# The key compare of the adjacency tiles reads its ramp from PSUM instead of SBUF

## What is computed

```python
h = typed_linear(feat[src], W, etype)
att = jax.nn.sigmoid(jax.nn.leaky_relu(h_l + h_r, NEG_SLOPE)) * edge_weight[:, None]
msg = h3.transpose(0, 2, 1) * att[:, None, :]
agg = jax.ops.segment_sum(msg, dst, num_segments=n_nodes)
```

```python
Wh = h @ W + b
base = adj_v * sc * no_diag            # one number per edge
prop_pos = segment_sum((base * sim_pos)[:, None] * Wc, row)
prop_neg = segment_sum((base * sim_neg)[:, None] * Wc, row)
out = scale * (coeff[0] * prop_pos + coeff[1] * prop_neg + coeff[2] * Wh)
```

## Time and profile before

| | |
|---|---|
| time, median of 3 runs | 4748.81 us (4748.74 to 4754.69) |
| profiled execution: its own time | 4738.92 us |
| profiled execution: its span | 4736.4 us |
| TensorE busy | 3146.4 us (66%) |
| VectorE busy | 3140.1 us (66%) |
| GpSimd busy | 3231.1 us (68%) |
| ScalarE busy | 1567.6 us (33%) |
| mean granted TensorE clock | 0.844 of 2.4 GHz |

### The profile page before, as it was taken

The page is one execution under the profiler, slowest core; times in us unless marked ns, Lnnn a source line. Parts: engine busy times, 40 slices in busy tenths (PEclk is TensorE's granted clock), DMA queues, the critical chain, the costliest instruction groups (busy, mean ns, idle before and its releaser), DMA issues. The chain is left out here.

```text
span 4736.4 us, 63536 instructions
## 1 busy us (share of the span) xinstructions
PE 3146.4 (66%) x16141; PEld 1881.8 (40%) x16141; DVE 3140.1 (66%) x5194; ACT 1567.6 (33%) x3248; POOL 3231.1 (68%) x3224
## 2 busy tenths in 40 slices
PE   2576777777777777776555655555476767676778
PEld 2344454554455455444343443444232222322222
DVE  4677776767777677775655555554477767676787
ACT  2422232323232232323411211221344545444434
POOL 0277777777777777775377777777676777775546
PEclk6798888988888888897877777777689989889999
DMA  1233333323233332333322222222355545455556
GB/s 53 97 92 97 91 96 91 101 88 99 91 95 94 91 98 91 98 92 88 103 66 72 78 66 71 80 68 66 112 156 143 163 128 163 134 156 140 177 163 191
DMA packets 355160, 502.05 MB, mean 106 GB/s; under 512 B 92987, under 2 KB 214844, under 8 KB 354669
## 3 DMA queue, kind: packets, MB, share of 16 engines
q1 hardware_dynamic: 251549, 394.52, 25.3%
q0 software_dynamic: 100352, 102.96, 10.7%
q10 hardware_dynamic: 2896, 0.59, 0.1%
HBM read 290.63 MB, written 207.16 MB: 105 GB/s over the span
## 5 line engine op out<-in xcount | busy, mean ns | idle before, releaser
L809 POOL DMA_INDIRECT frows<-messages,fidx x2352 | 2280.6, 970 | 847.8 <-issue 669.3
L889 PE MATMUL fps_b<-hot_key,hot_lo 128*128 128x343 f32 x3136 | 1238.6, 504 | 406.4 <-PEq L70 403.7
L948 DVE TENSOR_TENSOR strip<-strip,fps_b 128x343 f32 x1568 | 787.7, 502 | 546.1 <-DVEq L70 521.6
L824 ACT ACTIVATE turned<-fps_t 128x512 f32<-128x512 f32 (+1 forms) x754 | 431.6, 572 | 1742.7 <-ACTq L70 1738.1
L879 PE MATMUL fps_sum<-hot,frows 128*64 128x80 f32 x4704 | 551.5, 302 | 600.1 <-PEq L70 600.1
L1118 POOL DMA_INDIRECT lrows<-messages,lidx x784 | 743.3, 948 | 294.5 <-issue 222.6
L889 PEld LDWEIGHTS fps_b<-hot_key,hot_lo 128*128 128x128 f32 x3136 | 544.8, 207 | 728.3 <-issue 676.3
L879 PEld LDWEIGHTS fps_sum<-hot,frows 128*64 128x64 f32 x4704 | 522.8, 195 | 691.1 <-issue 691.1
L918 DVE TENSOR_SCALAR hot_key<-iota_f,edge 128x343 f32<-128x343 f32 x1574 | 753.2, 479 | 0.1
L1284 ACT ACTIVATE pos<-l_c,coeff 128x896 f32<-128x896 f32 x392 | 394.4, 1006 | 597.6 <-PE l_c L1179 596.8
L1179 PE MATMUL l_c<-unit_t,unit_g 64*128 64x448 f32 x1568 | 437.2, 636 | 133.5 <-DVE acc L1107 72.4
(11 more groups left out here) (183 smaller groups left out, 1880.0 us busy)
## 6 DMA issues: line engine op xcount, KB each, us to landing
adj<-turned SPq DMA_DIRECT2D x696, 256.0 KB
edge<-adj SPq DMA_DIRECT2D x294, 448.0 KB
adj_x<-adj SPq DMA_DIRECT2D x98, 448.0 KB
frows<-messages,fidx POOLq DMA_INDIRECT x2352, 2.4
messages<-msg SPq DMA_DIRECT2D x14, 1120.0 KB, 4.6
lrows<-messages,lidx POOLq DMA_INDIRECT x784
adj<-turned SPq DMA_DIRECT2D x58, 64.0 KB
wh_g<-wh_rows SPq DMA_DIRECT2D x56, 32.0 KB, 1.7
```

The lines of the kernel that those rows point to most:

```text
L809: pool.indirect_dma_start(rows[:, q, k, :], None, tab_l[l].ap(), bass.IndirectOffsetOnAxis(ap=idx[:, q, k:k + 1], axis=0)).then_inc(s_got[ ...
L824: act.activation(turned[j][:, 0:(b - a) * P], ps_t[j][:, 0:(b - a) * P], ACT.Copy).then_inc(s_t_free, 1)
L889: pe.matmul(ps_b[n % KB][:, 0:NT * TWIN], hot_lo[:, s % 2, k, :], hot_key[:, n % KB, :], start=True, stop=True).then_inc(s_b, 1)
L948: dve.tensor_tensor(part, part, ps_b[n % KB][:, 0:NT * TWIN].rearrange("p (h w) -> p h w", w=TWIN), ALU.add).then_inc(v, 1)
```

## The change

`ps_iota` is filled with all 343 columns of the ramp in place of 128, in the same bank, and the key compare reads it there. The output `hot_key` stays in SBUF, and the two scalars still come from `edge` in SBUF. The order of the instructions is the same on every engine, and no wait is added or taken away.

```diff
-                    dve.tensor_copy(ps_iota[:, 0:P], iota_f[:, 0:P]).then_inc(s_iota, 1)
+                    dve.tensor_copy(ps_iota[:, 0:NT * TWIN], iota_f[:, :]).then_inc(s_iota, 1)
...
-                        dve.tensor_scalar(hot_key[:, n % KB, :], iota_f[:, :], edge[:, A_KEY, bass.ds(at, 1)], edge[:, A_BASE, bass.ds(at, 1)],
+                        dve.tensor_scalar(hot_key[:, n % KB, :], ps_iota[:, 0:NT * TWIN], edge[:, A_KEY, bass.ds(at, 1)], edge[:, A_BASE, bass.ds(at, 1)],
                                           ALU.is_equal, ALU.mult).then_inc(s_key, 1)
```

## The result

The changed kernel takes 4773.47 us (median of 4 runs, 4767.97 to 4778.45), the kernel before 4748.77 us: a ratio of 1.0054, 95% interval 1.004 to 1.0069. (The ratios further down are taken against the kernel before as it was timed beside those runs, 4746.90 or 4745.91 us.) It is slower, as forecast, but by 24.7 us where I forecast 79. The profiled execution has a span of 4765.7 us, 29.3 us more than before.

The account below looks back on a forecast made before the run. GpSimd's gather pace bounds both calls, the VectorE-TensorE loop nearly level with it in the first. Profiled 4738.9 + 87 (first call) - 7.5 (second) = 4818 us; with 9.9 for the median, 4828 us; range 4745 to 4905.

Parts of the forecast that it names:

- GpSimd as the bound, in both calls: In both `fast_path` calls GpSimd's gathers set the pace before the change, 17.9 us for each edge row.
- The gain in the second call: GpSimd stays the bound in `fast_path(1)` and loses its disturbance by keys: 7.5 us less.
- GpSimd would begin to wait for buffers in the first call: After the change GpSimd waits for free buffers in `fast_path(0)`, whose length becomes about 2099 us.
- The key's price: VectorE's key compare loses its double rate with a PSUM source: +0.178 us each, 0.37 to 0.55.
- The rule that I had taken from the errata section: Vector operations: fixed 58 cycles from SBUF, 120 from PSUM; about 0.065 us more a key, 58 us in the sum.
- The lengthening of the key to 0.64 us: Some VectorE keys run longer beside a gather; reading PSUM ends this, taking 0.027 us off each key.
- L809's mean: GpSimd's gathers, no longer disturbed by keys, fall from a mean of 970 to about 958 ns.
- 894 keys on the path, 135 us: First call: 282 of 1176 keys are covered by waits; the other 894 cost 0.151 us each, 135 us.
- From that comes off the wait for gathered rows that the slower loop no longer meets, 48 us.: First call: VectorE's visible waits for gathered rows, 48 us, are subtracted as slack, leaving 87 us more.
- The rival on the clock: TensorE's clock falls in the first call, row sums lengthen, 62 us more: 4890 us; chance 0.16.
- The rival that GpSimd stays the bound: A key costing only +0.05 us leaves both calls at GpSimd's pace, 29.5 us faster: 4719 us; chance 0.11.
- point of decision: Key cost of 0.09 us, below which the kernel isn't slower, worked out over 894 first-call keys.

Follow-up runs that it names:

- second_only: Kernel before, with the key compare reading its ramp from PSUM in the second call alone; 4733.93 us, ratio 0.9973.
- half_before: Kernel before, with GpSimd issuing only 7 of a row's 14 gathers and the key unchanged; first call 1889.64 us.
- stt_psum: Changed kernel, with the key from PSUM written as a two-source operation with one scalar and base as second source; 4718.05 us, ratio 0.9946.
- first_only: Kernel before, with the key compare reading its ramp from PSUM in the first call alone; 4779.47 us, ratio 1.0073.
- half_after: Changed kernel, with GpSimd issuing only 7 of a row's 14 gathers; first call 2021.75 us.

## Why the prediction was right or wrong

- **GpSimd as the bound, in both calls.** Right: with half the gathers the first call fell to 1889.6 us and the second to 664.8. The gain in the second call, 7.5 us by the count of disturbed gathers, was 9.7 (and 10.3 in second_only). I had also forecast that GpSimd would begin to wait for buffers in the first call; VectorE fell behind it by up to 45 us, from a row's last gather to its scaling (10 us in the kernel before), but the call ended before GpSimd had to wait for more than 0.2 us.
- **The key's price.** Right: +0.178 us, from 0.37 to 0.545, 628 ns. The lengthening of the key to 0.64 us, and that of the gathers beside it, went away.

  The rule that I had taken from the errata section of the page "VectorE: DVE Perf Modes" of the Trainium skill, by which the sum would have been 58 us larger, isn't borne out: 567 ns from PSUM and 568 from SBUF, and the 0.545 us are the 0.367 and the lost half of the rate, with nothing over.
- **L809's mean.** Forecast 958 ns, found 966. The gathers that overlap a key and no scaling now carry 1.5 us beyond the median in place of 29.5, but those that overlap a row scaling carry 51 in place of 32. This is what GpSimd's gain in the first call came to: 21 us fewer beside the keys and 22 more beside the row scalings. It cost nothing here, since GpSimd was no longer the bound in that call. Its cause is open.
- **894 keys on the path, 135 us.** The total was right (132 us), the reasoning only in part. How many keys are covered is no fixed number: the first 0.118 us cost 56.5 us, the next 0.060 us 75.6, and 168 keys cost 20 or 64 us, depending on their place. So the agreement of the total was luck. TensorE's clock appears to be part of the answer for the two places; for the steps it is open.
- **"From that comes off the wait for gathered rows that the slower loop no longer meets, 48 us."** This is the step that failed. It was 87 to 101 us. The visible wait was 48 us (60 with small gaps and the keys that gathers lengthened). Of the rest, most stood in the waits for TensorE, whose row sums met the low clock more often (62 of 111 over 3 us, 47 without the waits for gathers, 22 with something to do in front of them), some in front of the `hot_lo` compares (7 us), and up to 13.5 us was VectorE's own work. It explains the miss: 135 - 101 - 7.5 is 26.5 us, and 24.7 were measured; with 87 in place of 101 the keys cost 118 us, and the 31 us between them stay.
- **The rival on the clock.** It had the right actor and the wrong sign. TensorE's row sums became shorter in the first call, 343.40 to 320.82 us of busy time (3.09 to 2.89 us each), not longer:

```profile
222.55:2246.25 2023.70, 320.82 (x3108) 303.36 (x3108) 0.88 0.31 92
```

  The slower keys took away the waits for gathered rows, and with them some of the long row sums: 49 of the 111 still last over 3 us. I had taken the second call, with its 3.64 us, as the picture of a loop with more idle time, when it is the picture of a loop that waits for gathers. Without those waits, in half_before, its row sums take 137.17 / 55 = 2.49 us:

```profile
2240.58:2905.39 664.81, 137.17 (x1540) 129.18 (x1540) 0.93 0.28 86
```
- **The rival that GpSimd stays the bound.** Its point of decision, 0.09 us a key, was too low, since it was worked out from the same 48 us. At 0.118 us, stt_psum is 0.5% faster than the kernel before, and 16.8 us of waits for gathered rows are left in its first call. The changed kernel passed the point, but by less than I thought.

## What to carry to other kernels

Here a source moved from SBUF to PSUM cost a one-source float32 operation its double rate (0.367 to 0.545 us for 343 columns) and took the operation out of GpSimd's way (337 disturbed gathers beside a key, then one). Which of the two counts depends on who bounds the stretch, so decide it stretch by stretch: the same edit gained 0.3% of the kernel in one call and lost 0.7% in the other. Where a loop waits for an outside supplier, its slack is not the sum of the waits with the supplier's name: what idles behind them can run at a lower clock, and that part is booked elsewhere; to know the slack, take the supplier away and time the loop. And count scalars: the same key with one per-partition scalar instead of two, the other number read as a second source, occupied VectorE for 0.485 us in place of 0.545, which was enough to turn the loss into a gain.

## What I had not expected of the hardware

- Two useless products of 343 columns in front of each wait of TensorE, some 1.3 us of extra work at the high clock, made a loop-bound call 51 us shorter (2023.70 to 1972.68 us), with the mean granted clock going from 0.88 to 0.94. By then GpSimd was the bound again (1972.68 - 1495.50 = 477.2 us), so the loop itself may have gained more. Even in the kernel before, whose first call GpSimd bounds, they saved 13 us.
- The loop's answer to VectorE's time is uneven in a way that repeats: 2023.7, 2021.8 and 2021.8 us for the first call in three kernels with the same long key (the changed kernel, first_only and half_after), but 20 or 64 us for the same 30 us of added work at two places.
- A per-partition scalar costs about 0.06 us of occupied time at 343 columns. This is an estimate from three different operations with a source in PSUM: `tensor_scalar` with two scalars takes 0.545 us, `scalar_tensor_tensor` with one 0.485, the strip add with none 0.42.
